# Nucleus attention in a four-layer graph network on one core: ties judged in the sorted values, one refinement loop nest, twelve blocks a loop, 250-column maxima in step 1

## Chip, cores and metric

One core of a Trainium2 chip runs the whole program. The metric is the device time of one execution in microseconds (us). Engines are named as in the profile: PE is the matrix engine, ACT the scalar engine, DVE the vector engine, POOL the GpSimd engine, SP the engine that issues most transfers.

## What is computed

Four graph layers over 5000 nodes with 128 features, each followed by a residual sum and a layer norm. The change lies in layer 1 alone, which makes two attention steps. Of the reference, what matters:

```python
def _top_p_attention(X, W1, W2, W3):
    q = X @ W1.T @ W2.T
    k = X @ W3.T
    logits = q @ k.T / TAU                     # 5000 x 5000
    probs = softmax(logits, axis=-1)
    idx = argsort(-probs)                      # largest first
    sp = take_along_axis(probs, idx)
    cs = cumsum(sp)
    keep_sorted = cs - sp < TOP_P              # 0.9
    A = probs * mask(keep_sorted)
    return A / A.sum(-1)
for n in range(2):
    A = _top_p_attention(Xa, W1, W2, W3)
    Xf = R @ Xf ; Xa = A @ Xa
    Z = Z + Xf @ U1[n].T + Xa @ U2[n].T
```

A row keeps its largest probabilities until they hold 0.9 of the mass. Where several probabilities equal the smallest one that is kept, only as many of them stay as the rule wants; the others of the same value have to be dropped. In step 2 such equal values are common, because rows of A that kept a single entry in step 1 make exact copies of rows of Xa.

## The kernel before

`attention_step` (line 507) is called twice: "s0" (line 1130) with `rounds` 1, and "s1" (line 1137) with `rounds` 3. Here they are called step 1 and step 2. Each treats 40 blocks of 125 queries; a block's 5000 exponentials lie in one of three buffers (`work`, DEPTH = 3). In step 2 the queries are sorted so that those with small norm come first.

**PE** does in its step b: the transposes and products of `attend(b - 1)` (lines 623 and 631), which wait for `s_kept`, the mark that block b - 1 is masked; then the logits of block b + 2 (line 616); then 40 products of the diffusion term (line 651). **ACT** moves the transposed pieces to `turned` (729), copies the logits (714), and takes the exponentials of block b + 1 (719, 720), in that order.

**DVE** does for each block: `maxima(b + 1)`, which is 40 MAX8 instructions, each the 8 largest of 125 columns, into a list of 320 candidates (801), and their maximum (803); then `search(b)`; then `keep(b)`.

- `search` (847) narrows a threshold with passes over the 320 candidates (`mass_above`, line 808), sorts the values of the last narrow interval 8 at a time (880 to 885; 8 values in step 1, 24 in step 2), and lets `least_kept` (825) find the smallest kept value `found`. A row is open when the sorted values don't reach the goal, or `found` lies below `reach`, the largest of the eighth maxima of the pieces (889). `gather_flags` (812) folds the flags of 125 rows to one number in seven small instructions, the last of them at line 822; a register load (845) and a branch (894) follow.
- If a row is open, `refine` (970) runs on the whole block: three bisections over the 5000 columns (973), new candidates (926), five bisections over the candidates, at the end the 8 largest values of the interval (`least_in_bracket`, 940), then the flags again. The code has it twice in each step, once after the first branch, once in a loop of 13 rounds (900) whose rounds load the flag again and skip the body.
- `keep` (1029) masks the block with one pass over 5000 columns (1031), whose accumulator gives the kept mass. From that mass it works out how many equal values have to go (1033 to 1044), gathers flags a second time (1045) and loads them. With 1 or more to drop a MATCH_REPLACE8 over the block takes up to 8 of them out (1048), with 9 or more a second one runs (1051), with 17 or more `drop_ties` (997) counts them along the row (1013 to 1025, each twice).

The DVE loop (1068) holds three blocks and turns 13 times; block 39 stands behind it.

Of the kernel before, what the change touches and what calls it, by code (L numbers as in the profile page):

```python
# [64 lines left out]
CANDIDATE_BISECTIONS = (4, 1)  # L65
MORE_ROUNDS = 13
# [3 lines left out]
def gnn_kernel(nc, x, adj_tiles, adj_wide, h0, yT, w1T, w2T, w3T, u1T, u2T, ln_g, ln_b,  # L70
# [3 lines left out]
    with ExitStack() as ctx:  # L74
# [432 lines left out]
        def attention_step(name, v_diffuse, v_attend, raw_diffuse, raw_attend, steps, rounds, lead, arranged):  # L507
# [4 lines left out]
            with ExitStack() as c1:  # L512
# [15 lines left out]
                cands = [wt[0:P, 1336:1656], pair[0:P, 0:8 * NB], cols[0:P, 80:80 + 8 * NB]]  # L528
                neg_max = [cols[0:P, 400 + k:401 + k] for k in range(DEPTH)]
                total = [cols[0:P, 404 + k:405 + k] for k in range(DEPTH)]  # L530
                windows = wt[0:P, 1656:1656 + 8 * NB]
# [240 lines left out]
                def _(v):  # L772
# [11 lines left out]
                    is_open = flags[0:P, 0:1].bitcast(I32)  # L784
                    v.memset(flags, 0.0)
                    v.memset(merged, 0.0)
                    v.memset(zeros, 0.0)
                    v.memset(vals, 0.0)
                    for k in range(WINDOW):
                        v.memset(ordinal[:, k:k + 1], float(k + 1))  # L790
# [53 lines left out]
                    def any_open():  # L844
                        return v.value_load(undecided, min_val=0, max_val=WINDOW // 8)

                    def search(par):
# [34 lines left out]
                        for r in range(1, rounds):  # L882
# [10 lines left out]
                        first = any_open()  # L893
                        with v.If(first > 0):

                            mass_above(cand, windows, hi, base)
                            refine(w, cand)
                            second = any_open()
                            with v.If(second > 0):
                                with v.Fori(0, MORE_ROUNDS):  # L900
                                    more = any_open()
                                    with v.If(more > 0):
                                        refine(w, cand)
# [22 lines left out]
                    def candidates_up_to_hi(w, cand):  # L926

                        for half in range(2):
# [4 lines left out]
                            for c in range(NB // 2):  # L933
                                at = 8 * (half * NB // 2 + c)
                                v.max(cand[:, at:at + 8], scratch[:, c * P:(c + 1) * P])
# [34 lines left out]
                    def refine(w, cand):  # L970


                        for _ in range(BISECTIONS):
                            bisect(w, dump, goal)
# [5 lines left out]
                        for n in CANDIDATE_BISECTIONS:  # L980
                            if n != CANDIDATE_BISECTIONS[0]:
                                lower_hi(cand)
                            for _ in range(n):
                                bisect(cand, windows, rest)
                            least_in_bracket(cand)
# [3 lines left out]
                        v.scalar_tensor_tensor(out=flags[0:P, 0:1], in0=found, scalar=reach,  # L989
                                               in1=flags[0:P, 0:1], op0=ALU.is_lt, op1=ALU.max)  # L990
# [4 lines left out]
                        gather_flags()  # L995
# [794 lines left out]
```

## Time and profile before

| | us |
|---|---|
| median of 3 runs | 8053.71 (8051.28 to 8060.34) |
| the profiled execution | 8054.94 |
| its span, first to last instruction | 8052.3 |

| engine | busy us | share |
|---|---|---|
| DVE | 5737.6 | 71% |
| PE (matmul) | 4855.3 | 60% |
| ACT | 2295.8 | 29% |
| POOL | 290.3 | 4% |

The DVE part of step 1 runs from 959 to 2412 us of the span, that of step 2 from 2738 to 5898 us. Times in a timeline are us from the span's start; the bracket at a line's end is the idle time of the engine before it and what ended it, where "issue" means that nothing in the profile was waited for (register loads, branches and the fetch of code lie in it). A group of instructions is merged in one row with its count.

### The profile page before, as it was taken

Reading aid. Unit: us, or ns where it says so; the run is one execution under the profiler, and the core shown is the slowest. Engines: PE = TensorE matmul, PEld = TensorE weight load, DVE = VectorE, ACT = ScalarE, POOL = GpSimd, SP = SyncE. Lnnn points to the kernel's source line nnn. Section 1 sums busy time; section 2 is a strip of 40 time slices with the busy share of each in tenths; the row PEclk is TensorE's granted clock in tenths of the full one; section 3 lists DMA queues with packets and bytes.
Section 4 is the critical chain, followed back from the end, with each engine's and each line's share of the span. In section 5 each row is a group of like instructions: output and inputs, shape, how many; then the busy total and the mean of one; then the engine's idle time right before and its main releaser. Section 6 shows DMA issues by size and latency. Waiting matters only on the chain. (4 is left out here: it accounts for less than half of the span.)

```text
span 8052.3 us, 90545 instructions
## 1 busy us (share of the span) xinstructions
PE 4855.3 (60%) x27532; PEld 3333.2 (41%) x27532; DVE 5737.6 (71%) x14206; ACT 2295.8 (29%) x3252; POOL 290.3 (4%) x170
## 2 busy tenths in 40 slices
PE   6998698888875512321335456763322788872982
PEld 2443377777764312211224345552221222221982
DVE  4777266767671487888887877778825799994774
ACT  2333254444441101110112223332211322211642
POOL 0000000000002000000000000000000022220000
PEclk9999699999987756665667778886666999995996
DMA  4442121111101200000001111100010333320860
GB/s 144 149 149 95 57 82 70 68 68 71 74 28 59 87 13 14 26 26 13 26 26 40 39 39 52 52 28 2 2 39 14 112 108 107 107 80 27 296 215 26
DMA packets 194733, 550.19 MB, mean 68 GB/s; under 512 B 19663, under 2 KB 81762, under 8 KB 183962
## 3 DMA queue, kind: packets, MB, share of 16 engines
q1 hardware_dynamic: 189098, 541.17, 18.8%
q0 software_dynamic: 5120, 3.97, 0.2%
q14 instruction: 415, 3.40, 0.1%
q8 instruction: 100, 1.64, 0.1%
HBM read 525.77 MB, written 19.24 MB: 68 GB/s over the span
## 5 line engine op out<-in xcount | busy, mean ns | idle before, releaser
L623 PE MATMUL ps<-ident,arena 125*125 125x125 f32 x3200 | 537.5, 301 | 2067.1 <-DVEq L1055 2067.1
L623 PEld LDWEIGHTS ps<-ident,arena 125*125 125x125 f32 x3200 | 467.3, 214 | 2083.6 <-issue 1664.7
L729 ACT ACTIVATE turned<-ps 125x500 f32<-125x500 f32 x800 | 466.6, 586 | 2633.3 <-PE ps L623 2633.3
L1330 DVE SCALAR_TENSOR_TENSOR arena<-arena,pair 125x1000 f32<-125x1000 f32 x800 | 939.3, 1255 | 71.3 <-ACT arena L1293 71.3
L631 PE MATMUL ps<-arena,turned 125*125 125x129 f32 x6400 | 903.3, 288 | 7.8 <-ACT turned L729 7.8
L1348 PE MATMUL ps<-arena 125*64 125x500 f32 x3200 | 763.9, 601 | 193.9 <-DVE arena L1330 193.9
L631 PEld LDWEIGHTS ps<-arena,turned 125*125 125x125 f32 x6400 | 829.9, 200 | 19.3 <-ACT turned L729 12.5
L651 PE MATMUL ps<-arena 125*125 125x129 f32 x6400 | 761.0, 279 | 86.0 <-DMA arena<-in_adj_tiles 85.6
L651 PEld LDWEIGHTS ps<-arena 125*125 125x125 f32 x6400 | 736.8, 191 | 150.0 <-DMA arena<-in_adj_tiles 82.0
L616 PE MATMUL ps<-arena,wt 64*125 64x500 f32 x1600 | 716.7, 601 | 9.6 <-ACT wt L706 6.5
L1031 DVE SCALAR_TENSOR_TENSOR arena<-arena,wt 125x5000 f32<-125x5000 f32 x80 | 434.1, 5427 | 379.0 <-issue 379.0
L714 ACT ACTIVATE arena<-ps 125x500 f32<-125x500 f32 x800 | 469.6, 587 | 262.4 <-PE ps L616 262.4
L1348 PEld LDWEIGHTS ps<-arena 125*64 125x64 f32 x3200 | 197.8, 137 | 757.0 <-DVE arena L1330 526.2
L616 PEld LDWEIGHTS ps<-arena,wt 64*125 64x125 f32 x1600 | 296.6, 189 | 375.0 <-issue 341.1
L206 PE MATMUL ps<-arena 128*125 x800 | 402.7, 586 | 65.0 <-DVEq L231 65.0
L239 DVE TENSOR_TENSOR arena<-arena,ps 125x500 f32<-125x500 f32 x400 | 270.1, 676 | 234.5 <-PE ps L206 168.0
L213 PE MATMUL ps<-arena 125*128 125x500 f32 x800 | 403.2, 585 | 2.2 <-DVE arena L239 2.2
L1293 ACT ACTIVATE arena<-arena 125x2000 bf16<-125x2000 f32 x100 | 186.4, 1871 | 694.3 <-DVE arena L1330 577.8
L801 DVE MAX8 wt<-arena 125x8 f32<-125x125 f32 x1120 | 217.2, 273 | 204.2 <-ACT arena L714 177.3
L1432 PE MATMUL ps<-arena 125*125 125x129 f32 x3200 | 355.8, 274 | 10.9 <-DVE arena L1419 10.9
L1432 PEld LDWEIGHTS ps<-arena 125*125 125x125 f32 x3200 | 355.6, 189 | 11.7 <-DVE arena L1419 11.7
L266 ACT ACTIVATE arena<-arena 125x500 f32<-125x500 f32 x400 | 247.0, 620 | 397.1 <-DVE arena L239 397.0
(325 smaller groups left out, 6341.8 us busy)
## 6 DMA issues: line engine op xcount, KB each, us to landing
arena<-in_adj_wide SPq DMA_DIRECT2D x400, 500.0 KB, 4.5
arena<-in_adj_tiles SPq DMA_DIRECT2D x400, 488.3 KB
arena<-in_adj_wide SPq DMA_DIRECT2D x80, 1250.0 KB, 5.4
x_saved<-arena SPq DMA_DIRECT2D x4, 2500.0 KB
arena<-x_saved SPq DMA_DIRECT2D x2, 2500.0 KB
arena<-att_saved SPq DMA_DIRECT2D x1, 2519.5 KB
arena<-in_x SPq DMA_DIRECT2D x1, 2500.0 KB
arena<-in_h SPq DMA_DIRECT2D x1, 2500.0 KB
```

What stands on the lines that cost most here:

```text
L206: pe.matmul(gram[:, c % 2, :], y_rows[:, c * P:(c + 1) * P], y_rows[:, bass.ds(s * GW, GW)], start=True, stop=True).then_inc(s_gram, 1)
L213: pe.matmul(agg, nodes(VA, FA)[:, c, 0:F], chunk(c), start=(c == 0), stop=(c == NB - 1))\
L616: pe.matmul(bank_logit[g % 4], query[par], rows(KT + g * GW, GW, ATT), start=True, stop=True).then_inc(s_logit, 1)
L623: mm = pe.transpose(banks_turn[:, g % 2, c * P:(c + 1) * P], work[par][:, j:j + P], ident[0:P, 0:P])
L631: mm = pe.matmul(acc_attend, turned[:, g % 2, c * P:(c + 1) * P], nodes(v_attend, FA)[:, j, :], start=(j == 0), stop=(j == NB - 1))
L651: mm = pe.matmul(acc_diffuse, ring[:, j * P:(j + 1) * P], nodes(v_diffuse, FA)[:, j, :], start=(j == 0), stop=False)
L714: a.activation(work[par][:, g * GW:(g + 1) * GW], bank_logit[g % 4], ACT.Copy).then_inc(s_copied, 1)
L729: a.activation(turned[:, g % 2, :], banks_turn[:, g % 2, :], ACT.Copy)\
L1031: v.scalar_tensor_tensor(out=w, in0=w, scalar=found, in1=w, op0=ALU.is_ge, op1=ALU.mult, accum_out=kept_mass)
L1330: v.scalar_tensor_tensor(out=weight(m).rearrange("p (g w) -> p g w", g=2), in0=rows(ERB + h * N + r * PASS, PASS).rearrange("p (g w) -> p ...
L1348: mm = pe.matmul(ps[64 * t:64 * t + 64, q, 0:GW], flat_v[:, at:at + 64], weight(m + t)[:, g * GW:(g + 1) * GW], start=(c == 0), stop=(c == ...
L1432: mm = pe.matmul(acc(g)[:, k, :], weight(m)[:, k * P:(k + 1) * P], nodes(v_at, FA)[:, c, :], start=(c == 0), stop=(c == NB - 1))
```

## The change

- **Ties from the sorted values.** `search` ends in a new function `judge`. It counts, in the sorted values, those that are at or above `found` though the mass before them already reaches the goal (`dropped_count`), and writes the values to be replaced (`needles`). `keep` no longer works them out from the kept mass: behind the masking pass it goes at once to the replacement (always in step 2, in step 1 only where the flag says so).
- **One flag per block.** Each row has six verdicts; the largest of all rows is the block's number. 3: refine. 2: replace and then run `drop_ties`. 1: replace (step 2: a second time). Verdict 2 is given where `found` does not exceed `reach`, where the last of the sorted values is at or above `found`, where more than 16 are to be dropped, and, after a refinement, where the candidates hold more values equal to `found` than the 8 sorted ones show. The second gathering of flags, in `keep`, goes away; the load and the branch stay, on the number that `search` or `refine` left.
- **One refinement copy.** `refine` stands once in each step, inside two nested loops of four rounds, each with its own load of the flag; its bisections are loops too.
- **Twelve blocks per loop.** The DVE loop holds twelve blocks and turns three times; blocks 36 to 39 stand behind it.
- **250-column maxima in step 1.** MAX8 takes 250 columns there, 20 per block, and the candidate list has 160 entries instead of 320. Step 2 keeps 125 columns and 320 entries.

The diff, cut to its core:

```diff
-BISECTIONS = 3 ; CANDIDATE_BISECTIONS = (4, 1) ; MORE_ROUNDS = 13
+BISECTIONS = 3 ; CANDIDATE_BISECTIONS = 4 ; REFINE_ROUNDS = 4
@@ attention_step: span is new
+                CANDS = 8 * N // span
+                cands = [wt[0:P, 1336:1336 + CANDS], pair[0:P, 0:CANDS], cols[0:P, 80:80 + CANDS]]
@@ maxima
-                            for c in range(g * GC, (g + 1) * GC):
-                                v.max(cands[par][:, 8 * c:8 * c + 8], work[par][:, c * P:(c + 1) * P])
+                            for c in range(g * GW // span, (g + 1) * GW // span):
+                                v.max(cands[par][:, 8 * c:8 * c + 8], work[par][:, c * span:(c + 1) * span])
@@ search
                         least_kept(goal, 8 * rounds)
-                        v.scalar_tensor_tensor(out=flags[0:P, 0:1], in0=found, scalar=reach,
-                                               in1=flags[0:P, 0:1], op0=ALU.is_lt, op1=ALU.max)
+                        v.tensor_scalar(verdicts[:, 4:5], vals[:, 8 * rounds - 1:8 * rounds], found, 2.0,
+                                        ALU.is_ge, ALU.mult)
+                        judge(goal, 8 * rounds)
+
+                    def judge(aim, width):
+                        v.scalar_tensor_tensor(out=dropped[:, 0:width], in0=sums[:, 0:width], scalar=aim,
+                                               in1=vals[:, 0:width], op0=ALU.is_ge, op1=ALU.mult)
+                        v.tensor_scalar(verdicts[:, 0:1], flags[0:P, 0:1], 3.0, None, ALU.mult)
+                        v.tensor_scalar(verdicts[:, 1:2], found, reach, 3.0, ALU.is_lt, ALU.mult)
+                        v.tensor_scalar(verdicts[:, 2:3], found, reach, 2.0, ALU.is_le, ALU.mult)
+                        v.drain()
+                        v.scalar_tensor_tensor(out=counts[:, 0:width], in0=dropped[:, 0:width], scalar=found,
+                                               in1=zeros[:, 0:width], op0=ALU.is_ge, op1=ALU.max,
+                                               accum_out=dropped_count)
+                        v.drain()
+                        v.tensor_scalar(needles[:, 0:16], ordinal[:, 0:16], dropped_count, found, ALU.is_le, ALU.mult)
+                        if rounds > 1:
+                            v.tensor_scalar(verdicts[:, 3:4], dropped_count, 8.0, None, ALU.is_gt)
+                            v.tensor_scalar(verdicts[:, 5:6], dropped_count, 16.0, 2.0, ALU.is_gt, ALU.mult)
+                        else:
+                            v.tensor_scalar(verdicts[:, 3:4], dropped_count, 0.0, None, ALU.is_gt)
+                        v.drain()
+                        v.tensor_reduce(flags[0:P, 0:1], verdicts, AX.X, ALU.max)
                         v.drain()
                         gather_flags()
@@ refine
-                        for _ in range(BISECTIONS):
+                        with v.Fori(0, BISECTIONS):
                             bisect(w, dump, goal)
...
+                        with v.Fori(0, CANDIDATE_BISECTIONS):
+                            bisect(cand, windows, rest)
+                        least_in_bracket(cand)
+                        lower_hi(cand)
+                        bisect(cand, windows, rest)
+                        least_in_bracket(cand)
...
+                        v.scalar_tensor_tensor(out=windows, in0=cand, scalar=found, in1=cand, op0=ALU.is_equal,
+                                               op1=ALU.mult, accum_out=equal_near)
+                        v.drain()
+                        v.scalar_tensor_tensor(out=counts[:, 0:8], in0=vals[:, 0:8], scalar=found, in1=vals[:, 0:8],
+                                               op0=ALU.is_equal, op1=ALU.mult, accum_out=equal_shown)
                         mass_above(cand, windows, hi, base)
+                        v.tensor_scalar(verdicts[:, 4:5], equal_near, equal_shown, 2.0, ALU.is_gt, ALU.mult)
+                        judge(rest, 8)
@@ drop_ties: the quota is reckoned from dropped_count instead of a fixed 16
@@ keep: masking pass, then
+                        if rounds > 1:
                             v.match_replace(w, needles[:, 0:8], w, 0.0)
                             v.drain()
+                        ties = worst()
+                        with v.If(ties > 0):
+                            at = 8 if rounds > 1 else 0
+                            v.match_replace(w, needles[:, at:at + 8], w, 0.0)
+                            v.drain()
+                            with v.If(ties > 1):
+                                drop_ties(w)
@@ step
                         search(u)
+                        first = worst()
+                        with v.If(first > 2):
+                            mass_above(cand, windows, hi, base)
+                            with v.Fori(0, REFINE_ROUNDS):
+                                second = worst()
+                                with v.If(second > 2):
+                                    with v.Fori(0, REFINE_ROUNDS):
+                                        more = worst()
+                                        with v.If(more > 2):
+                                            refine(w, cand)
                         keep(u)
+                    ROUND = 4 * DEPTH
+                    ROUNDS = (NB - 1) // ROUND
+                    with v.Fori(0, ROUNDS) as k:
+                        for u in range(ROUND):
+                            step(k * ROUND + u, u % DEPTH)
+                    for b in range(ROUNDS * ROUND, NB):
+                        step(b, b % DEPTH, ahead=b + 1 < NB)
```

## Rows read from the trace of the kernel before

**Rows 1.** Busy time by stretch: steps 1 and 2; PE, PEld, DVE, ACT, POOL, clock
```profile
959.00:2440.00 1481.00, 1279.33 (x8795) 1071.18 (x8793) 1013.54 (x4005) 683.30 (x1017) 0.00 (x0) 0.94 0.17 67
2737.00:5900.00 3163.00, 1260.15 (x8111) 1046.37 (x8112) 2548.62 (x7783) 670.72 (x1000) 54.28 (x76) 0.69 0.07 26
```
**Rows 2.** Waits of DVE in step 2: total us, times, longest
```profile
DVE arena L1031 <- issue: 203.8, 40, 15.5
DVE pair L801 <- issue: 58.6, 12, 7.2
...
DVE wt L801 <- issue: 7.8, 13, 0.6
...
DVE wt L1062 <- ACT arena L720: 3.5, 1, 3.5
```
**Rows 3.** Waits of PE for masked blocks, 1021 to 2220 us, step 1
```profile
PE ps L623 <- DVEq L1055: 120.1, 24, 10.7
```
**Rows 4.** The mark that a block is masked (L1055), step 1: first and last start
```profile
L1055 DVEq DRAIN  x40: 19/19/89, 987.6 to 2412.0; - x40
```
**Rows 5.** Timeline of PE in step 1: two attends, logits and diffusion between
```profile
1053.58 1.03 PE L623 MATMUL ps<-ident,arena 125*125 125x125 f32 x8
...
1067.63 8.64 PE L616 MATMUL ps<-arena,wt 64*125 64x500 f32 x20
1076.20 9.12 PE L651 MATMUL ps<-arena 125*125 125x129 f32 x80
...
1085.38 1.03 PE L623 MATMUL ps<-ident,arena 125*125 125x125 f32 x8
```
**Rows 6.** Timeline of ACT in the same PE step: the exponentials
```profile
1077.39 4.45 ACT L720 ACTIVATE arena<-arena,cols 125x5000 f32<-125x5000 f32 x1
```
**Rows 7.** Timeline of DVE in step 1, block 2 and what follows
```profile
1045.25 7.69 DVE L801 MAX8 wt<-arena 125x8 f32<-125x125 f32 x40 [1.60 <-ACT arena L714]
...
1062.33 0.55 DVE L876 SCALAR_TENSOR_TENSOR wt<-cols,wt 125x320 f32<-125x320 f32 x1
...
1063.02 0.49 DVE L880 MAX8 wt<-wt 125x8 f32<-125x320 f32 x1
...
1064.86 0.22 DVE L889 SCALAR_TENSOR_TENSOR wt<-wt 125x1 f32<-125x1 f32 x1
...
1066.17 0.17 DVE L822 TENSOR_REDUCE icols<-wt 1x1 int32<-1x32 f32 x1
1070.62 5.43 DVE L1031 SCALAR_TENSOR_TENSOR arena<-arena,wt 125x5000 f32<-125x5000 f32 x1 [4.28 <-issue]
...
1078.30 0.17 DVE L822 TENSOR_REDUCE icols<-wt 1x1 int32<-1x32 f32 x1
1085.44 7.69 DVE L801 MAX8 pair<-arena 125x8 f32<-125x125 f32 x40 [6.97 <-issue]
```
**Rows 8.** The same engine, step 2, one refined block: end of refining, masking, replacing
```profile
3386.04 0.17 DVE L822 TENSOR_REDUCE icols<-wt 1x1 int32<-1x32 f32 x1
3389.74 5.43 DVE L1031 SCALAR_TENSOR_TENSOR arena<-arena,wt 125x5000 f32<-125x5000 f32 x1 [3.53 <-issue]
```
**Rows 9.** The same, a block refined twice: masking after 12 empty rounds
```profile
2996.28 5.42 DVE L1031 SCALAR_TENSOR_TENSOR arena<-arena,wt 125x5000 f32<-125x5000 f32 x1 [15.50 <-issue]
```
**Rows 10.** The same, block 5: second replacement, end of `drop_ties`, next block
```profile
3506.66 5.35 DVE L1051 MATCH_REPLACE8 arena<-wt,arena 125x5000 f32<-125x5000 f32 x1
...
3536.02 2.82 DVE L1025 SCALAR_TENSOR_TENSOR arena<-arena,wt 125x2500 f32<-125x2500 int16 x1
3542.32 3.90 DVE L801 MAX8 pair<-arena 125x8 f32<-125x125 f32 x20 [3.48 <-issue]
```
**Rows 11.** Lines 1051, 1013, 975 alone: count, duration ns, first and last start
```profile
L1051 DVE MATCH_REPLACE8 arena<-wt,arena x26: 5349/5351/5353, 2830.9 to 5892.0; 125x5000 f32<-125x5000 f32 x26
...
L1013 DVE TENSOR_SCALAR arena<-arena,wt x6: 1514/1519/1523, 3513.1 to 5757.7; 125x2500 int16<-125x2500 f32 x6
...
L975 DVE COPY wt<-wt x19: 153/154/155, 2776.2 to 5683.7; 125x1 f32<-125x1 f32 x19
```

More of the change, by code:

```diff
@@ L64 @@
 BISECTIONS = 3
-CANDIDATE_BISECTIONS = (4, 1)
-MORE_ROUNDS = 13
+CANDIDATE_BISECTIONS = 4
+REFINE_ROUNDS = 4
 LIGHT = 0.55
@@ L505, in _, with attention_step @@
                     v.drain()
-        def attention_step(name, v_diffuse, v_attend, raw_diffuse, raw_attend, steps, rounds, lead, arranged):
+        def attention_step(name, v_diffuse, v_attend, raw_diffuse, raw_attend, steps, rounds, span, lead, arranged):
             with ExitStack() as c1:
@@ L788, in _ @@
                     v.memset(vals, 0.0)
+                    v.memset(verdicts, 0.0)
                     for k in range(WINDOW):
@@ L842, in just_below_hi, with worst @@
                         v.drain()
[L844 to L845 removed]
+                    def worst():
+                        return v.value_load(undecided, min_val=0, max_val=3)
                     def search(par):
@@ L891, in search @@
                         v.drain()
                         gather_flags()
[L893 to L903, printed above, removed]
@@ L932, in candidates_up_to_hi @@
                             v.drain()
-                            for c in range(NB // 2):
-                                at = 8 * (half * NB // 2 + c)
-                                v.max(cand[:, at:at + 8], scratch[:, c * P:(c + 1) * P])
+                            for c in range(HALF // span):
+                                at = 8 * (half * HALF // span + c)
+                                v.max(cand[:, at:at + 8], scratch[:, c * span:(c + 1) * span])
                             v.drain()
@@ L1002, in drop_ties @@
                         v.memset(last_rank, -1.0)
-                        v.scalar_tensor_tensor(out=above, in0=found, scalar=-16.0, in1=kept_mass,
-                                               op0=ALU.mult, op1=ALU.add)
-                        v.drain()
-                        v.tensor_tensor(above, above, goal, ALU.subtract)
+                        v.tensor_tensor(above, kept_mass, goal, ALU.subtract)
+                        v.tensor_scalar(removed, dropped_count, 16.0, 1.0, ALU.min, ALU.add)
                         v.drain()
@@ L1009, in drop_ties @@
                         v.drain()
-                        v.tensor_scalar(quota, quota, -1.0, None, ALU.add)
+                        v.tensor_tensor(quota, quota, removed, ALU.subtract)
                         for half in range(2):
@@ L1064, in step @@
                         search(u)
+                        first = worst()
[8 more added lines that the diff above has]
+                                            refine(w, cand)
                         keep(u)
+                        v.drain().then_inc(s_kept, 1)
+                    ROUND = 4 * DEPTH
+                    ROUNDS = (NB - 1) // ROUND
                     maxima(0, 0)
-                    with v.Fori(0, NB // DEPTH) as k:
-                        for u in range(DEPTH):
-                            step(k * DEPTH + u, u)
-                    step(NB - 1, (NB - 1) % DEPTH, ahead=False)
+                    with v.Fori(0, ROUNDS) as k:
[3 more added lines that the diff above has]
+                        step(b, b % DEPTH, ahead=b + 1 < NB)
         def mix_in(name, n, att_at, diff_at, h_at):
```

41 lines of the change are left out of this document (8 added, 33 removed).

## Prediction

> **What bounds the kernel now.** I read the busy time by stretch first, then who waits for whom in each step, then the timelines of DVE and PE through single blocks. In step 2 (3163 us of the span) DVE is busy 81% of the time and PE 40% [rows 1], and DVE's list of waits names another engine once, for 3.5 us; all else is "issue": register loads, branches and code on the way [rows 2]. So step 2 is DVE's own sequence of instructions, and each us taken from or put on it moves the end by as much. Step 1 is different. DVE sets the end there too, but PE is close behind: between 1021 and 2220 us PE waits only 120 us for masked blocks, 24 times [rows 3], and where it doesn't wait its attends start 1085.38 - 1053.58 = 31.8 us apart [rows 5]. DVE masks a block every (2412.0 - 987.6) / 39 = 36.5 us, the long first period, which the lead-in of PE holds up, included [rows 4].
>
> **Step 1, what DVE gains per block.**
> - Maxima: 40 MAX8 take 7.69 us, 0.192 each. MAX8 over 320 columns lasts 0.49, over 125 it lasts 0.273 by the page, so 1.1 ns per column; 250 columns make 0.192 + 0.14 = 0.33, twenty 6.7 us: -1.0 [rows 7].
> - Half the candidates: a pass over 320 lasts 0.55 and one over 5000 5.43, so 160 fewer save 0.17; seven `mass_above`, one window pass, one MAX8 and one reduction: -1.7 [rows 7].
> - `keep`: from the end of the masking pass (1076.05) to the end of the second gathering (1078.47) it is 2.4 us, which goes. The open flag in `search` (0.22 and its drain) goes: -0.3 [rows 7].
> - `judge` is not in the trace. It has nine instructions in four groups with a drain behind each. The like of them (one-column and 24-column operations in lines 1033 to 1042) take four groups and 1.3 us; I take 1.8, bounds 1.2 and 2.4.
> - Back jumps: the one shown idles DVE 6.97 us [rows 7], a turn without one 0.6 [rows 2]; ten of twelve go, 64 us or 1.6 per block.
> - Sum: 36.5 - 1.0 - 1.7 - 2.4 - 0.3 + 1.8 - 1.6 = 31.3 us with the long first period, and less without it.
>
> That is under PE's 31.8, so PE takes over. The exponentials of block b + 1 end 28.3 us after attend(b - 1) starts (1077.39 + 4.45 - 1053.58) [rows 5, 6], and search and keep need 22.4 us more, so DVE can run up to 2 x 31.8 - 50.7 = 13 us ahead of PE; that reserve swallows the two back jumps that are left. The first attend starts one such period before the second, at 1021.9; the lead-in of PE (logits and diffusion) sets it, and DVE's first block is long done. Attend(36) then starts at 1021.9 + 36 x 31.8 = 2167. Behind it PE has no diffusion and at last no logits, and DVE sets the end: exponentials of 38 at 2195, then two times 22.4 us: last block masked near 2242 to 2245 where it is 2412 now [rows 4]. **Step 1: -168 us**, bounds -130 (DVE still last in many blocks) and -175.
>
> **Step 2, the number of equal values.** After a refinement only 8 sorted values are shown. Verdict 2, and with it `drop_ties`, falls on a block where the candidates of one row hold more copies of `found` than are shown. Of the 40 blocks 16 are refined, 13 once and 3 twice (19 in all), and 3 run `drop_ties` now (line 1013 runs six times, twice per block); 26 make a second replacement [rows 11]. Going through the timeline block by block, 12 of the 16 refined blocks make the second replacement, so they have a row with 9 or more copies to drop: 8 sorted values can't show them, and all 12 must get verdict 2. For the other four I worked the rows out from the reference's inputs in single precision, with the rules of `search` and `refine`. This gives the trace's number of refinements and of replacements in all 80 blocks, and in each of the four there are rows with 14 or 20 equal values (these are copies of one node). So all 16 get verdict 2. The same working shows no refinement and no tie in step 1, with 250 columns either: `found` is never below 1.8 times `reach`. And no other block of step 2 gets verdict 2.
> - `drop_ties` lasts from 3512.0 to 3538.8, less one group of the quota: 26.5 us [rows 10]. 13 new blocks x 26.5 = **+345**.
> - Four of them make a second replacement that they don't make now: 4 x 5.5 [rows 11] = **+22**.
>
> **Step 2, the loop nest.** A load and branch take about 1.0 us, an empty round with its back jump 15.50 / 12 = 1.3 [rows 9]. A block refined once enters over two more loads (+2.0) and leaves over 3 + 3 empty rounds (7.8), where it now skips the second copy in 3.5 [rows 8]: +6.3. One refined twice leaves over 2 + 3 rounds, 6.6 instead of 15.5, and saves a load between: -7.5. 13 x 6.3 - 3 x 7.5 = **+60**.
>
> **Inside a refinement.** Two bisection loops add five taken back jumps and two exits. A taken one costs about 0.4 by the empty rounds, less their load; together +2.4, bounds 1 and, if each jump fetched code anew, 14. Two passes for the equal values, a verdict and `judge`, less the old flag: +2.4. 19 x 4.8 = **+91**.
>
> **Every block of step 2.** -2.4 for the gathering, -0.3 for the flag, +1.8 for `judge`: 40 x -0.9 = **-36**, bounds -60 and -12. The first replacement runs in all 40 now and after. The back jump costs 58.6 / 12 = 4.9 us against 0.6 at the other turns [rows 2]; ten of twelve go: **-43**. The skip of the refinement code, with its load, idles DVE 3.5 to 6.1 us in blocks that are not refined, 4.7 on the mean of 24; it varies with the place in the loop of three, and the long waits stand at the first place, behind the back jump. The skipped piece shrinks from two copies to one. One copy alone costs 3.53 now [rows 8], so I take **-10**, bounds +34 and -89 (a skip that costs the load alone).
>
> The Trainium skill (Runtime: NRT & Kernel Launch, section Instruction fetch mechanics) says that a taken branch whose target lies outside the window of code on the engine forces a fetch of it, and that the window is two blocks of 256 instructions. The skip in the rows passes some 240 instructions and costs 2.6 us more than its load, so the trace does not agree that the whole of such a window lies ahead; the new copy has some 215. By the rule the new skips would be free; that is the third rival.
>
> **The sum.** Step 2: 345 + 22 + 60 + 91 - 36 - 43 - 10 = +429. Step 1: -168. The profiled execution took 8054.94 us (2.6 outside its span), 1.2 above the median of three. 8054.9 + 429 - 168 = 8316, and I keep it for the median: **8316 us, 3.3% slower**.
>
> **The rivals.**
> - *The other side: `drop_ties` stays rare.* If verdict 2 comes in the 3 blocks of now alone, 345 + 22 go and the change gives 8316 - 367 = 7949. It turns at four: without new blocks the change gains 106 us, and each costs 26.5. For it speaks that step 2 otherwise pays only in the refined blocks; against it the 12 blocks with two replacements, of which 9 are new. Chance 0.04.
> - *DVE stays last in step 1.* If every skip costs 6.1 and `judge` 2.4, the DVE period comes to 33.3 and step 1 gains only 130 (+38); step 2 loses 44 at the skips and 24 at `judge`: 8316 + 106 = 8422. With half of it: 8370. For it: the first place in the loop costs 6 now. Against it: the second and third cost 3.5. Chance 0.10.
> - *The skip gets free.* One short copy might lie in what is fetched. Step 1 gains nothing, PE has it; step 2 gains 89 where I took 10: 8237. Chance 0.07.
> - *The 250 columns open rows in step 1.* Each refined block there adds some 65 us, and few of them hide. Against it stands the factor 1.8. Five such blocks make 8600. Chance 0.01.
>
> **Chances and range.** Forecast 0.78, its own range 8260 to 8370 (`judge` alone moves 36 us either way, the loops 20, the skips 30). To hold 8 in 10 with the two middle rivals partly in: 8238 to 8385. A difference under about 0.2%, 16 us, is all that a measurement of this kernel can't tell from none. Slower 0.95, faster 0.04 (the first rival), same 0.01 (a count of some four new blocks, out of the forecast's share).
>
> **What would show it.** In the profile after: line 1013's successor runs 32 times instead of 6 and the second replacement 30 times instead of 26; refinements stay 19; PE's attends in step 1 stand 31.8 us apart with hardly a wait for DVE, and its last block is masked near 2243 instead of 2412; step 2 is some 430 us longer. It is wrong if the count of `drop_ties` is not 16, if a block of step 1 refines, or if the empty rounds or the loops inside a refinement fetch code at each turn.

## The result, and the profile after

The changed kernel takes 8290.97 us (median, 8289.58 to 8308.67). The kernel before, run beside it, takes 8057.02. The ratio is 1.0294, with a 95% interval of 1.0276 to 1.0312: 2.9% slower, where 8316 us and 3.3% were forecast. The profiled execution took 8291.24 us with a span of 8289.5, against a span of 8052.3 before.

Busy time by stretch of the kernel after (columns as in [rows 1]): step 1, step 2, and the lead-in of step 2.

```profile
957.00:2265.00 1308.00, 1247.89 (x8796) 1043.74 (x8794) 874.15 (x3165) 673.29 (x1017) 0.00 (x0) 0.98 0.19 75
2572.00:6136.00 3564.00, 1263.16 (x8112) 1049.28 (x8113) 2920.56 (x8225) 671.14 (x1000) 55.96 (x76) 0.67 0.06 23
2555.00:2573.00 18.00, 12.62 (x17) 4.85 (x16) 7.87 (x38) 9.75 (x12) 0.00 (x0) 0.50 0.13 52
```

Blocks are numbered through both steps in this part: 0 to 39 are those of step 1, 40 to 79 those of step 2, so block 5 of step 2 in [rows 10] is block 45 here.

Against [rows 1] PE runs as many matmuls in both steps; in step 1 they are busy 31 us less, at a granted clock of 0.98 instead of 0.94. DVE lost 139 us of busy time in step 1, where PE is now busy 95% of the stretch, and gained 372 us in step 2. Next stands the mark that a block is masked in step 1 (line 1082 after, [rows 4] before) and who waited for it; then, for the whole run, line 1029 (a half block of `drop_ties`), line 1057 (the second replacement) and line 990 (one refinement), which answer to [rows 11].

```profile
L1082 DVEq DRAIN  x40: 19/19/89, 982.5 to 2237.8; - x40
...
  PE ps L624: 12.5, 2
...
L1029 DVE TENSOR_SCALAR arena<-arena,wt x32: 1514/1520/1523, 2681.1 to 5999.1; 125x2500 int16<-125x2500 f32 x32
L1057 DVE MATCH_REPLACE8 arena<-wt,arena x30: 5349/5351/5353, 2674.8 to 6127.7; 125x5000 f32<-125x5000 f32 x30
L990 DVE COPY wt<-wt x19: 152/154/154, 2614.8 to 5920.0; 125x1 f32<-125x1 f32 x19
```

The last block of step 1 is masked 174 us earlier (2412.0 before), and PE waits for masked blocks 12.5 us in all of step 1, for two of them, where the kernel before has 165.0 and 29 (in the stretch of [rows 3] 5.7 us instead of 120.1). In step 2 `drop_ties` runs in 32 / 2 = 16 blocks, not 3; second replacements went from 26 to 30, refinements stayed 19. PE's attends in step 1 start 31.85 us apart on the mean of 36, each 31.7 to 32.0; the two below, with the logits and the diffusion between, stand 1338.10 - 1306.10 = 32.0 us apart:

```profile
1306.10 1.03 PE L624 MATMUL ps<-ident,arena 125*125 125x125 f32 x8
...
1320.35 8.64 PE L617 MATMUL ps<-arena,wt 64*125 64x500 f32 x20
1328.92 9.12 PE L652 MATMUL ps<-arena 125*125 125x129 f32 x80
1337.88 0.38 PE L656 MATMUL ps<-arena,ident 125*125 x2
1338.10 1.03 PE L624 MATMUL ps<-ident,arena 125*125 125x125 f32 x8
```

DVE's timeline in step 2 of the kernel after, block 48: the flag, the masking pass behind the empty rounds, both replacements, `drop_ties`, the next block's maxima.

```profile
3987.02 0.17 DVE L826 TENSOR_REDUCE icols<-wt 1x1 int32<-1x32 f32 x1
3995.50 5.42 DVE L1048 SCALAR_TENSOR_TENSOR arena<-arena,wt 125x5000 f32<-125x5000 f32 x1 [8.07 <-issue]
...
4001.09 5.35 DVE L1052 MATCH_REPLACE8 arena<-wt,arena 125x5000 f32<-125x5000 f32 x1
...
4007.29 5.35 DVE L1057 MATCH_REPLACE8 arena<-wt,arena 125x5000 f32<-125x5000 f32 x1
4013.53 1.52 DVE L1029 TENSOR_SCALAR arena<-arena,wt 125x2500 int16<-125x2500 f32 x1
...
4036.47 2.82 DVE L1041 SCALAR_TENSOR_TENSOR arena<-arena,wt 125x2500 f32<-125x2500 int16 x1
4039.68 7.69 DVE L805 MAX8 pair<-arena 125x8 f32<-125x125 f32 x40 [0.39 <-issue]
```

After the second replacement ends (4012.64) the block needs 26.6 us more for `drop_ties`. The skip behind one refinement is now 8.07 us of empty rounds, where one skipped copy cost 3.53 [rows 8]. DVE's waits in step 2 (total, times, longest) answer to [rows 2]:

```profile
DVE arena L1048 <- issue: 218.0, 40, 8.8
DVE wt L923 <- issue: 66.3, 114, 2.1
...
DVE pair L805 <- issue: 14.4, 12, 3.6
```

Line 923 opens a bisection: of the 114 = 19 x 6 waits five per refinement are back jumps of the new loops inside `refine`, and the first of the six is the entry over two more loads. The back jumps (line 805) went from 58.6 to 14.4 us.

Where the 237.2 us of span came from, end to end. Here and below a value per block is the mean over the blocks of its kind in the profiled execution, if it is not given for one block.

| stretch | before | after | difference | forecast |
|---|---|---|---|---|
| to the first search of step 1 | 959.6 | 957.3 | -2.3 | 0 |
| first search to last mask, step 1 | 1452.5 | 1280.5 | -172.0 | -168 |
| last mask to first search of step 2 | 325.6 | 334.6 | +9.0 | 0 |
| first search to last mask, step 2 | 3160.0 | 3560.9 | +400.9 | +429 |
| behind step 2 | 2154.6 | 2156.2 | +1.6 | 0 |

### The profile page after: what moved, and what is told of

Same layout as the page of the kernel before. It is cut to its first block and busy times, and to the rows that moved or that the text cites. A ratio compares the mean times of both kernels' runs of the same rounds, so it can differ in the third digit from the quotient of the medians.

```text
span 8289.5 us, 90663 instructions
## 1 busy us (share of the span) xinstructions
PE 4832.0 (58%) x27532; PEld 3309.5 (40%) x27532; DVE 5969.3 (72%) x13770; ACT 2286.1 (28%) x3252; POOL 292.0 (4%) x170
## 3 DMA queue, kind: packets, MB, share of 16 engines
q8 instruction: 101, 1.65, 0.1%
## 5 line engine op out<-in xcount | busy, mean ns | idle before, releaser
L624 PE MATMUL ps<-ident,arena 125*125 125x125 f32 x3200 | 519.4, 294 | 2312.8 <-DVEq L1082 2312.8
L721 ACT ACTIVATE arena<-arena,cols 125x5000 f32<-125x5000 f32 x80 | 355.9, 4449 | 0.0
```

The source lines that it names most:

```text
L624: mm = pe.transpose(banks_turn[:, g % 2, c * P:(c + 1) * P], work[par][:, j:j + P], ident[0:P, 0:P])
```

## The experiments

The theory: step 1 became as fast as PE lets it, step 2 pays for `drop_ties` in every refined block, and the rest is small change of the loops. The rival reasons were that DVE is still the bound of step 1, and that part of the cost of step 2 is code fetched at the new jumps. Each ratio is to the kernel before, run beside it.

### `drop_ties` after a refinement left out

The kernel leaves out the exact dropping behind a refinement: the verdict for hidden copies makes only the second replacement.

```diff
-v.tensor_scalar(verdicts[:, 4:5], equal_near, equal_shown, 2.0, ALU.is_gt, ALU.mult)
+v.tensor_scalar(verdicts[:, 4:5], equal_near, equal_shown, 1.0, ALU.is_gt, ALU.mult)
```

> The changed kernel, but the verdict for more equal candidates than the sorted values show gives 1 instead of 2. Left out: the exact dropping of equal values in the 16 refined blocks of step 2 (drop_ties); their second replacement still runs. Theory (drop_ties costs 26.4 us a block, all of it on DVE's path): 16 x 26.4 = 423 us less, so 8291 - 423 = 7868, and step 2 comes to 3561 - 423 = 3138 us. Rival (the loss of step 2 lies in the nest, the loops and the fetch of code, and drop_ties is partly hidden by PE's work): 200 us less or so, 8090.

Measured: 7869.67 us, ratio 0.9762 (0.9742 to 0.9781). DVE in step 2, busy time by stretch:

```profile
2568.00:5720.00 3152.00, 1262.43 (x8114) 1048.61 (x8115) 2507.19 (x7969) 671.89 (x1000) 54.96 (x76) 0.69 0.07 26
```

DVE's busy time falls by 2920.6 - 2507.2 = 413 us, and step 2 from 3560.9 to 3147.7, by 413 as well; 16 x 26.4 = 423 was what the blocks hold, with the short gaps between their instructions. The skips of unrefined blocks took 0.4 us more each, 24 x 0.4 = 10, which leaves 413 for the step. So step 2 is DVE's sequence throughout, and the one verdict costs more than the whole change loses.

### Step 1 without the refinement code

```diff
-                        first = worst()
-                        with v.If(first > 2):
+                        if rounds > 1:
+                            first = worst()
+                            with v.If(first > 2):
...
```

> The changed kernel without load, branch and refinement code in step 1, which step 1 never enters on these inputs. It takes 4.6 us of idle time per block from DVE. Theory (PE is last in step 1, its blocks 31.8 us apart): step 1 moves by 0 to -10 us, 8281 to 8291, and DVE waits for the exponentials instead. Rival (DVE is still last in step 1): 38 x 3.7 = up to 140 us less, 8150.

Measured: 8299.3 us, 1.0294 (1.0277 to 1.0311): no change. First DVE's waits in step 1 of the changed kernel, then of this one:

```profile
DVE arena L1048 <- issue: 182.4, 40, 6.4
DVE wt L1068 <- ACT arena L721: 42.4, 17, 5.0
```

```profile
DVE wt L1068 <- ACT arena L721: 146.2, 40, 5.0
DVE cols L805 <- ACT arena L715: 41.0, 13, 25.2
```

The skips, 4.56 us per block, are gone. The waits for the exponentials (ACT, line 721) took their place, 40 instead of 17 of them, and the last block is masked at 2235.9 instead of 2237.8. From its first search step 1 took 1274.7 us instead of 1280.5. So step 1 of the changed kernel is bound by PE, whose logits ACT's exponentials need, and of the 182 us of idle time that DVE lost there at most 6 came through. Step 2 took 16 us more here (3576.8), 14 of it in its skips (4.39 us on the mean of 24 instead of 3.82), and the stretch between the steps 9 less, which is why the total stands still.

### 125 columns in step 1

```diff
-attention_step("s0", VA, VA, VB, VC, STEPS[0:6], 1, 2 * P, 3, False)
+attention_step("s0", VA, VA, VB, VC, STEPS[0:6], 1, P, 3, False)
```

> The changed kernel with MAX8 over 125 columns in step 1 as before (40 per block, 320 candidates). DVE gets 2.7 us more per block. Theory: DVE's own period goes from some 31.0 to 33.7 us and passes PE's 31.8, so step 1 grows by 2.1 x 38 = 80 us: 8371. If DVE had been last all along it would be 2.7 x 39 = 105 (8396); if PE has more room than thought, 20 or less (8311).

Measured: 8327.13 us, 1.0321 (1.0304 to 1.0338), about 22 us above the changed kernel where 80 was expected; its interval and that of the changed kernel overlap, so the reading rests on the step's own times. DVE's skips and waits in step 1, then PE's waits for masked blocks:

```profile
DVE arena L1048 <- issue: 124.8, 40, 6.1
...
DVE wt L1068 <- ACT arena L721: 8.5, 2, 4.9
```

```profile
PE ps L624: 38.4, 6
```

The search takes 1.5 us more per block and the maxima 1.2, and the waits for exponentials fall to two. But the skips fell from 4.56 to 3.12 us on the mean, though the code that is skipped has 20 MAX8 more. That leaves DVE a period of 32.3 us (masks of blocks 2 to 37), just above PE's 31.8, and its reserve ahead of PE takes most of the difference: PE's attends still start 31.8 us apart in the median, and PE waits for a mask in two blocks in the middle and in the last four. Step 1 ends 31 us later: its first attend starts 7.4 us later (1027.0; the runs kept here have 1015.7 to 1029.9), the next 36 take 7.5 more, and the blocks behind them, where DVE sets the end, 16.6. The size of the loss depends on where the code lies, not only on the work: there are 9 skips near 1.25 us, at other places of the loop than the 7 of the changed kernel, and the long ones are mostly 3.5 us where most were 4 to 6.

### Three blocks per loop

```diff
-                    ROUND = 4 * DEPTH
+                    ROUND = DEPTH
```

> The changed kernel with three blocks per DVE loop and 13 turns instead of twelve blocks and 3 turns. Theory: ten back jumps more in each step. Step 2: 10 x 3.4 to 4.3 = 34 to 43 us more. Step 1: DVE's mean period rises by 1.4 us to 32.4, over PE's 31.8, some 25 us more. Sum +65: 8356. Rival (a back jump only moves a fetch of code that the next skip would pay for anyway): +10 or less, 8300.

Measured: 8329.92 us, 1.0326 (1.0309 to 1.0343), about 26 above the changed kernel by the ratios, whose intervals just overlap, where 65 was expected: the part of step 2 came, that of step 1 hardly. DVE in step 2:

```profile
DVE pair L805 <- issue: 47.6, 12, 6.6
```

Step 2 takes 3603.4 us, 42.5 more, and of that 34 are the gaps before the maxima (17.8 to 52.1 us over all blocks). Step 1 ends only 8 us later, since DVE's reserve ahead of PE swallows most of its back jumps, as the prediction had it for two of them. The code of a block is the same here, and 9 of the 24 skips of step 2 are near 1.25 us, all at one of the three places of the loop. The profiled execution of this kernel, like that of the one with 125 columns, was some 20 us above its median, so the step times fit the ratios only to that.

### The bisections unrolled

```diff
-                        with v.Fori(0, BISECTIONS):
+                        for _ in range(BISECTIONS):
...
-                        with v.Fori(0, CANDIDATE_BISECTIONS):
+                        for _ in range(CANDIDATE_BISECTIONS):
```

> The changed kernel with the bisections of a refinement written out again instead of in two loops. Theory: a refinement loses five taken back jumps and two exits, 2.4 us by the prediction; 19 x 2.4 = 46 us less in the refinements; the skip gets some 75 instructions longer, which takes 10 to 20 back: 8260 to 8280 where the changed kernel has 8300. Rival (the loops are free, their jumps run beside the drains): 0 to +20.

Measured: 8348.97 us, 1.0357 (1.034 to 1.0374): slower by some 50 us, where 20 to 40 less was expected. A refinement did get shorter, from 64.88 to 62.98 us (-1.9). DVE's waits in step 2, and its timeline at block 45:

```profile
DVE arena L1048 <- issue: 314.0, 40, 36.7
DVE wt L923 <- issue: 30.4, 21, 2.0
```

```profile
3487.83 0.17 DVE L826 TENSOR_REDUCE icols<-wt 1x1 int32<-1x32 f32 x1
3524.93 5.43 DVE L1048 SCALAR_TENSOR_TENSOR arena<-arena,wt 125x5000 f32<-125x5000 f32 x1 [36.70 <-issue]
```

The waits at the bisections fell by 66.3 - 30.4 = 36 us, or 1.9 per refinement, which is the whole gain. The skips rose by 96. Of these, 56 are two blocks, 45 and 57, at the same place of the loop of twelve: there the six empty rounds take 36.9 us where they took 9.0. The DMA view between 3480 and 3530 us shows what DVE waited for:

```profile
q14 instruction: 18, 0.15, 1.2%
```

Eighteen packets of code in 50 us, one after the other. The trace has the loads and branches of these rounds too, which a timeline leaves out: the three inner rounds take 9.4 to 9.7 us each, nearly all of it waits of about 3.6, 3 and 2.4 us, and in every wait over 2 us one or two of the packets start; the last two outer rounds take 1.3 us each, and none starts in them. Another 38 us are the skips of unrefined blocks, 5.40 us on the mean of 24 instead of 3.82; none is near 1.2 any longer. The copy is some 75 instructions longer.

### A longer skip

```diff
                                             refine(w, cand)
+                                            with v.If(more > 7):
+                                                for _ in range(64):
+                                                    v.memset(verdicts, 0.0)
```

> The changed kernel with 64 small instructions behind a branch inside the refinement that is never taken on these inputs: nothing more is executed but one compare per refinement; the code that an unrefined block skips grows by 64 instructions and every block's code moves. Theory (a skip is short only where its target is already fetched, which depends on where the step lies in the code): no unrefined block of step 2 keeps a gap near 1.2 us, the mean gap of the 24 goes from 3.8 to 4.2 to 4.7 or more, 10 to 30 us more in step 2, nothing in step 1, where PE is last (if the mean gap reaches 6, 10 to 20 there). Rival (the gap depends on time or on transfers of other engines): the pattern of gaps stays as it is.

The number is never above 3, and the built program doesn't contain the branch (the trace has none of that line, and DVE executes exactly as many instructions of each kind as before), so this edit tests nothing: it is a repetition of the changed kernel. It gave 8295.71 us, 1.0291 (1.0274 to 1.0308), and what it shows is the spread. The 24 skips averaged 4.19 us instead of 3.82, with the short ones at the same blocks, so differences of some 10 us in the skips of a single profile say nothing. The stretch between the steps took 329.3 us here, where the changed kernel had 334.6 (more on that below).

### Hidden copies counted

After a refinement the hidden copies, (mass of all copies - mass of the shown ones) / `found`, are added to `dropped_count`, and verdict 2 comes only above 16.

```diff
+                        if hidden is not None:
+                            v.tensor_scalar(dropped_count, dropped_count, hidden, 0.25, ALU.add, ALU.add)
...
-                        v.tensor_scalar(verdicts[:, 4:5], equal_near, equal_shown, 2.0, ALU.is_gt, ALU.mult)
-                        judge(rest, 8)
+                        v.tensor_scalar(hidden, equal_near, equal_shown, quota, ALU.subtract, ALU.mult)
+                        v.memset(verdicts[:, 4:5], 0.0)
+                        judge(rest, 8, hidden)
```

> The changed kernel, but after a refinement the equal candidates that the 8 sorted values don't show are added to the number to be dropped (their mass over found, two small instructions and a reciprocal more), and verdict 4 is not given. Nothing is left out. Then drop_ties is needed only where more than 16 copies go: 3 blocks, as before the change, and the second replacement in 26 instead of 30. Theory: 13 x 26.4 + 4 x 5.6 - 19 x 0.6 = 354 us less than the changed kernel, 0.985 of the kernel before (some 7940). Rival (the loss lies in nest and loops): at most 200 less, still slower than before.

Measured: 7961.73 us, 0.9878 (0.9861 to 0.9894), where 0.985 was expected. It drops all hidden copies, which is too many in a row whose 8 shown copies don't reach the goal, so that part of the computation is changed; the second replacement ran 30 times and not 26, which fits the same reason. With `REFINE_ROUNDS` 2 in place of 4:

> e5_counted with two nested loops of two rounds instead of four (up to 4 refinements; the inputs need 2). Each of the 16 refined blocks leaves over four empty rounds less, 1.27 us each: 16 x 5.1 = 81 us less than e5_counted, 0.975 of the kernel before (some 7860). Rival (an empty round costs only its load, 0.55): 35 less.

Measured: 7884.64 us, 0.9781 (0.9762 to 0.98). The gap behind a block refined once is 3.3 us instead of 8.4, so a turn of an empty round costs 5.1 / 4 = 1.3 us, as before.

### The number to drop from the mass

This version does what `keep` did before, inside `refine`. The mass of the values above `found` plus that of all copies of `found` is known there, so the number of copies beyond the goal follows without seeing them. No part of the computation is left out.

```diff
+                        v.scalar_tensor_tensor(out=limits[:, 0:8], in0=vals[:, 0:8], scalar=found, in1=vals[:, 0:8],
+                                               op0=ALU.is_gt, op1=ALU.mult, accum_out=above)
+                        v.tensor_scalar(neg_found, found, -1.0, None, ALU.mult)
+                        v.drain()
+                        v.tensor_scalar(above, above, base, equal_near, ALU.add, ALU.add)
+                        v.drain()
+                        v.tensor_scalar(limits, ordinal, neg_found, above, ALU.mult, ALU.add)
...
+                            v.scalar_tensor_tensor(out=counts, in0=limits, scalar=aim, in1=zeros, op0=ALU.is_ge,
+                                                   op1=ALU.max, accum_out=dropped_count)
```

> The changed kernel, but a refinement counts the values to drop from the mass of the candidates above found and of all candidates equal to it, and no longer from the 8 sorted values; verdict 4 is not given after it. Nothing is left out. (e5_counted took every hidden copy as one to drop. In rows where all copies of a value span the interval some of the hidden ones stay, so it dropped too many there: a working of the rows in single precision gives 1 to 7 such rows in each refined block, and none for the count by mass.) Theory: drop_ties in 3 blocks, the second replacement in 26; the refinements take about as long as e5's. 13 x 26.4 + 4 x 5.6 - 10 = 355 less than the changed kernel, 0.985 of the kernel before; by e5, 0.988, less 4 x 5.6: 0.985. Rival (as with e5, the missing part of the gain goes into skips that lie elsewhere in the code): 0.990.

Measured: 7957.84 us, 0.9875 (0.986 to 0.989), between what was expected and its rival. Step 2 got 330.6 us shorter than in the changed kernel, where 355 was said; the skips of unrefined blocks took 4.79 us on the mean instead of 3.82, 23 us of the difference. With `REFINE_ROUNDS` 2:

> e9_by_mass with two nested loops of two rounds. Theory: 16 x 5.1 = 81 us less than e9, 0.975 of the kernel before (7860). Rival: skips of code elsewhere, 0.980.

Measured: 7874.54 us, 0.9768 (0.9755 to 0.9781): faster than both kernels. Of this last version, line 1041 (the half block of `drop_ties`), line 1069 (the second replacement) and the mark, over the whole run; then DVE behind a block refined once:

```profile
L1041 DVE TENSOR_SCALAR arena<-arena,wt x6: 1514/1519/1523, 3356.0 to 5587.4; 125x2500 int16<-125x2500 f32 x6
...
L1069 DVE MATCH_REPLACE8 arena<-wt,arena x26: 5349/5351/5352, 2672.1 to 5718.3; 125x5000 f32<-125x5000 f32 x26
...
L1094 DVEq DRAIN  x80: 19/19/115, 983.5 to 5723.9; - x80
```

```profile
2656.93 0.17 DVE L826 TENSOR_REDUCE icols<-wt 1x1 int32<-1x32 f32 x1
2657.18 0.16 DVE L1024 TENSOR_TENSOR wt<-wt 125x1 f32<-125x1 f32 x1
2660.29 5.42 DVE L1060 SCALAR_TENSOR_TENSOR arena<-arena,wt 125x5000 f32<-125x5000 f32 x1 [2.96 <-issue]
```

Both counts are those of the kernel before, 6 and 26, while the gains of step 1, of the second gathering and of the back jumps stay. Step 2 takes 3230.3 us with four rounds and 3150.0 with two, against 3160.0 in the kernel before, so nearly all that this version gains on the kernel before lies in step 1. The 80 us between them are the empty rounds, 16 blocks x 5.1 = 82.

### 250 columns alone

In the kernel before, step 1 takes its maxima over 250 columns and keeps 160 candidates; nothing else is changed.

```diff
-                            for c in range(g * GC, (g + 1) * GC):
-                                v.max(cands[par][:, 8 * c:8 * c + 8], work[par][:, c * P:(c + 1) * P])
+                            for c in range(g * GW // span, (g + 1) * GW // span):
+                                v.max(cands[par][:, 8 * c:8 * c + 8], work[par][:, c * span:(c + 1) * span])
```

> The kernel before with one part of the change alone: MAX8 over 250 columns and 160 candidates in step 1. DVE loses 2.7 us per block and comes from 36.0 to 33.3, still above PE's 31.8, so all of it shows: 38 x 2.7 = 103 us less, 0.987 of the kernel before, nothing in step 2. Rival (PE is last sooner, in the blocks between back jumps, which go from 33.6 to 30.9 there): 70 us less, 0.991. Third way (the refinement copies get shorter and the skips move): 20 either way.

Measured: 7979.0 us, 0.9898 (0.9882 to 0.9913). The mark of step 1, and who waited for it; then DVE's waits in step 1, first of the kernel before, then of this one:

```profile
L1056 DVEq DRAIN  x40: 19/88/115, 986.0 to 2335.6; - x40
...
  PE ps L624: 92.0, 14
```

```profile
DVE arena L1031 <- issue: 175.3, 40, 6.9
DVE pair L801 <- issue: 81.5, 12, 7.1
```

```profile
DVE arena L1032 <- issue: 165.5, 40, 6.9
DVE pair L802 <- issue: 127.6, 24, 8.6
...
DVE wt L1063 <- ACT arena L721: 3.8, 1, 3.8
```

The search is 1.65 us shorter and the maxima 1.2, 2.85 per block or 111 us over 39 blocks, but the last mask comes 76.4 us earlier. The time is nearer to that of the rival, PE last sooner, but the reason is not the rival's: DVE waits for exponentials once, ahead of block 1, so DVE is last all along and nothing of its gain is lost to PE. What takes the rest is DVE's own idle time where code is fetched. Behind each back jump a second wait of some 3 us stands now inside the row of MAX8, with one packet of code in each: 127.6 - 81.5 = 46 us more at the maxima, and 10 less at the skips. 111 - 46 + 10 = 75. That is the third way of the expectation, 36 us where 20 was said.

## Why the prediction came out near, point by point

- **The verdict on hidden copies: right.** 16 blocks were forecast for `drop_ties` and 30 second replacements, and both came. `drop_ties` costs 43.94 - 17.51 = 26.4 us per block (26.5 said), 13 x 26.4 = 344; the leaving out took 413 away. The first rival, that it stays rare, was off. Its price was not: 7949 us for a kernel with 3 such blocks, and 7957.84 with the number from the mass.
- **Step 1: right in size and reason.** Last mask at 2237.8, forecast 2242 to 2245, PE waiting for two blocks. The second rival, DVE still last, fell with the kernel that has no refinement code there. How close it was shows with 125 columns, where DVE's period came to 32.3 us and DVE was last in six blocks.
- **Every block of step 2: right.** The search, with `judge` in it, went from 16.15 to 17.87 us: 40 x 1.72 = +69, where 40 x (1.8 - 0.3) = 60 was said. The second gathering is worth 2.6 per block (`keep` went from 14.63 to 12.00 in blocks with one replacement), 2.4 said.
- **Back jumps: right.** 59.2 to 17.8 us over all gaps before the maxima, -41 where -43 was said.
- **The nest: right within a few us.** The gap behind one refinement went from 3.58 to 8.42 (+4.8; 6.3 was said with the two loads of the entry, which lie in the refinement's own time), behind two from 15.43 to 6.86 (-8.6; -7.5 with the load).
- **Inside a refinement: mis-sized.** A block refined once spends 64.88 - 59.43 = +5.45 us more there. The entry waits 0.8 + 1.7 where it waited 0.8, so 1.6 of it is the entry (2.0 said). The loops wait 5 times 0.36 and twice 0.23; written out, the same places still wait some 0.08 each, and the unrolled kernel puts the loops at 1.9 in all (2.4 said). What is left for the passes over equal values, the verdict and `judge` less the flag is 5.45 - 1.6 - 1.9 = 1.9, where 2.4 was said. So a refinement itself grew by 3.8 us and not 4.8, 72 us over 19 and not 91. With entries a little cheaper and exits a little dearer than said, the 16 refined blocks cost 132 us more before `keep`, where 60 + 91 = 151 was said. These 19 us and the 9 of the skips below are what the forecast for step 2 was too high by.
- **The skips: the third rival was partly true.** The 24 unrefined skips went from 4.62 to 3.82 us, -19 where -10 was taken and -89 was the rival. They are not one cost. Here is one of the short ones, block 54, in the kernel after:

```profile
4585.74 0.17 DVE L826 TENSOR_REDUCE icols<-wt 1x1 int32<-1x32 f32 x1
4587.18 5.43 DVE L1048 SCALAR_TENSOR_TENSOR arena<-arena,wt 125x5000 f32<-125x5000 f32 x1 [1.27 <-issue]
```

  Of the 24 gaps 7 are near 1.25 us, the load alone, and the others 3.5 to 7.0; six of the short ones stand at three places of the twelve, one in the code behind the loop. What the long ones wait for is, by the times, code: each of the 17 has one packet of the `instruction` queue in it, with the masking pass some 2 us behind the packet's start, and none of the 7 has one. The same holds in step 1 (33 long skips with packets, 7 short ones without) and in every other run kept here. The Trainium skill (Runtime: NRT & Kernel Launch, section Instruction fetch mechanics) says that a taken jump forces a fetch where its target lies outside a window of two blocks of 256 instructions. The skipped copy has some 215, so by that rule hardly a skip should fetch: the trace agrees in those 7 gaps and not in the other 17, and in the unrolled kernel, whose some 290 instructions are fewer than two blocks too, in none of the 24. So the place of the jump counts beside its length.
- **Between the steps: not foreseen, and not the change's doing.** The lead-in of step 2 took 9 us more with the same instructions. PE's timeline, kernel after:

```profile
2553.25 13.54 PE L617 MATMUL ps<-arena,wt 64*125 64x500 f32 x16
```

  The sixteen products take 0.85 us each, where twenty of the same shape take 8.64 (0.43). The granted clock is 0.50 from 2555 to 2573 us, the lower level of 1.2 GHz, behind 0.92 in the stretch from 2530 to 2555; before the change it was 0.87 in the like stretch. But the repetition of the changed kernel did not have it: from 2550 to 2568 us, the like stretch, its clock is 0.89, the block's products take the usual time,

```profile
2554.25 8.64 PE L617 MATMUL ps<-arena,wt 64*125 64x500 f32 x20 [0.60 <-ACT wt L707]
```

  and the steps lie 329.3 us apart. In the kernel with 125 columns the logits of two whole blocks ran slowly (17.02 us each), and the steps lay 347.3 us apart; over all runs it is 325.5 to 347.3. So the 9 us are spread between executions; why the clock falls in some was not tried. They make the total look nearer to the forecast than the two steps are, where it was 28 and 4 us too high.

The sum by measured terms for step 2: `keep` as a whole went from 20.19 to 26.70 us, 40 x 6.51 = +260 (344 for `drop_ties`, 4 x 5.6 = 22 for the second replacements, and -105, or 2.6 per block, for the gathering). The search adds 69, the refined blocks 13 x (5.45 + 4.84) + 3 x (8.1 - 8.6) = 132, the skips -19 and the back jumps -41: 401 in all, and 400.9 on the trace.

## What to carry to other kernels

Before one test takes the place of two, ask what the early one can see: here 8 sorted values stood for rows with 14 or 20 equal ones, and "more than I can see" had to take the costliest path in each of the 16 blocks that mattered; a sum that is at hand (the mass) gave the number for 0.5 us per refinement (65.36 against 64.88). Price an edit by the step in which its engine sets the end. DVE's savings in step 1 stop at PE's 31.8 us per block, and in step 2 every us counts. Give an empty round of a loop its price (1.3 us here) times all rounds that are turned in vain: two rounds instead of four gave 80 us back.

## What the runs showed of the hardware

- **A skip's cost goes by its place.** In step 2 the jump over the same code costs 1.2 us at three of twelve places in the loop and 3.5 to 7 at the others, in a repetition at the same blocks; with three blocks per loop it is short at one place of three. When the code gets longer other places are short (3.12 us on the mean of step 1 with 125 columns, 4.56 with 250) or none is (the unrolled bisections). In all thirteen profiles no skip under 1.6 us has a packet of code in it and every longer one has.
- **Empty rounds can fetch their code at each turn.** Six took 8.0 to 9.0 us in the changed kernel, 1.3 to 1.5 each. With 75 instructions more inside the skipped body they took 36.9 at one place of the twelve and 8.4 at the others, with 18 code packets in 50 us. Three inner rounds took 9.4 to 9.7 us each, and in every wait over 2 us of theirs one or two of the packets start. That packets and waits belong together is read from their times; it was not tried apart.
- **A near loop is cheap.** A turn of a bisection loop waits 0.36 us, the back jump over twelve blocks 3.5 to 3.6 us at the maxima of step 2 and 4.1 in step 1, and the one over three blocks up to 6.6 in step 2 (7.2 in the kernel before).
- **Shorter work can meet a fetch.** With 250 columns alone twelve waits of some 3 us came up inside the row of MAX8 of step 1, each with a packet of code, and took a third of the gain.
- **The clock of a short stretch differs between executions.** The same products at the start of step 2 took 0.85 us each at a granted clock of 0.50 in one execution of the changed program, and 0.43 at 0.89 in another.
